# Lookup of gate and up weights: one of the seven comparison masks of a unit moves from VectorE to GpSimd

## What is computed

```python
def _ghost_linear(x, idx, lut):
    w = lut[idx]
    return jnp.einsum('bsh,oh->bso', x, w)
gate = _ghost_linear(x, gate_idx, lut)      # gate_idx, up_idx: (688, 256), values 0 to 15
up = _ghost_linear(x, up_idx, lut)
h = jax.nn.silu(gate) * up
return _ghost_linear(h, down_idx, lut)      # down_idx: (256, 688)
...
x = x + 0.5 * _L0_ffn_ref(_layernorm(x), ...)
x = x + _L0_attn_ref(_layernorm(x), ...)
x = x + 0.5 * _L0_ffn_ref(_layernorm(x), ...)
```

## Time and profile before

| | us |
|---|---|
| median of three runs (533.44 to 533.71) | 533.71 |
| profiled execution, its own time | 530.59 |
| span of the profiled execution | 528.9 |
| DVE busy over the span | 375.0 |
| PE busy over the span | 475.3 |
| POOL busy over the span | 159.0 |
| DVE's first mask starts | 6.80 |
| last matmul of unit 3 ends | 35.98 |

### The profile page before, as it was taken

The page is one execution under the profiler, slowest core; times in us unless marked ns, Lnnn a source line. Parts: engine busy times, 40 slices in busy tenths (PEclk is TensorE's granted clock), DMA queues, the critical chain, the costliest instruction groups (busy, mean ns, idle before and its releaser), DMA issues.

```text
span 528.9 us, 17153 instructions
## 1 busy us (share of the span) xinstructions
PE 475.3 (90%) x7478; PEld 396.0 (75%) x7478; DVE 375.0 (71%) x739; ACT 285.7 (54%) x516; POOL 159.0 (30%) x215
## 2 busy tenths in 40 slices
PE   4999999999989988759889998999978799999996
PEld 3658797988978866647778777877856678898986
DVE  6998836466777998855778887788848856565542
ACT  3658535252447989876556655666545533233241
POOL 1100040204051111116556777656636401000000
PEclk9999999999999999778999999999989999999999
DMA  8950070000000000010000000000340000101011
GB/s 201 235 202 1 1 337 1 1 1 1 0 1 0 2 0 1 20 40 5 4 4 5 4 5 5 5 4 4 147 198 4 2 3 0 41 1 40 1 40 41
DMA packets 7163, 21.31 MB, mean 40 GB/s; under 512 B 688, under 2 KB 5296, under 8 KB 6448
## 3 DMA queue, kind: packets, MB, share of 16 engines
q1 hardware_dynamic: 6688, 18.05, 10.2%
q10 hardware_dynamic: 400, 2.16, 1.8%
HBM read 12.87 MB, written 6.55 MB: 37 GB/s over the span
## 4 chain that ended last, share of the span: by engine, by line
PE 39%; issue 11%; ACT 8%; POOL 7%; DVE 6%; DMA 0%; SPq 0%; POOLq 0%; DVEq 0%; ACTq 0%
POOL w L1229 5%; PE intra L994 4%; DVE cv L640 2%; PE seg L862 2%; ACT cv L678 2%; PE yo L68 2%; PE yo L69 2%; PE yo L70 2%; PE pj L68 1%; PE XB L956 1%; PE pj L70 1%; PE XB L916 1%; PE new L968 1%; PE pj L69 1%; ACT pre L677 1%
## 5 line engine op out<-in xcount | busy, mean ns | idle before, releaser
L1229 POOL TENSOR_TENSOR w<-xdt,ends 32x512 f32<-32x512 f32 (+3 forms) x63 | 66.5, 1074 | 2.8 <-PE prior L963 1.4
L1013 ACT ACTIVATE seg<-seg 128x512 f32<-128x512 f32 x64 | 35.9, 579 | 50.2 <-PE seg L862 50.0
L640 DVE SCALAR_TENSOR_TENSOR cv<-pre,vec,cv 128x512 f32<-128x512 f32 x72 | 52.9, 750 | 2.8 <-ACT cv L678 1.1
L1097 DVE TENSOR_TENSOR mmat<-seg,gs 128x512 f32<-128x512 f32 x64 | 42.5, 684 | 15.8 <-ACT seg L1013 15.8
L514 POOL TENSOR_TENSOR n_rstd<-n_ve,m_half 128x4 f32<-128x4 f32 x12 | 13.0, 1086 | 122.7 <-DVE n_ve L509 122.6
L1033 ACT ACTIVATE xbd<-xdt 32x512 f32<-32x512 f32 x64 | 39.9, 624 | 1.2
L68 PE MATMUL pj<-n_xT,win 128*128 128x512 f32 x88 | 35.6, 404 | 5.0 <-PEq L130 2.3
L994 PE MATMUL intra<-xbd,mmat 128*32 128x32 f32 x2048 | 34.5, 223 | 5.4 <-issue 5.4
L862 PEld LDWEIGHTS seg<-abk,m_seg 96*32 96x32 bf16 x2048 | 21.1, 97 | 23.7 <-DVE mmat L1097 12.8
L994 PEld LDWEIGHTS intra<-xbd,mmat 128*32 128x32 f32 x2048 | 32.2, 152 | 8.2 <-issue 6.2
L1026 ACT ACTIVATE f_hT<-f_h 128x512 fp32r<-128x512 f32 (+1 forms) x24 | 15.2, 632 | 41.0 <-DVE f_h L1108 41.0
(11 more groups left out here) (252 smaller groups left out, 1454.0 us busy)
## 6 DMA issues: line engine op xcount, KB each, us to landing
wgu_dram<-wgu SPq DMA_DIRECT2D x1, 2816.0 KB, 8.2
wgu<-wgu_dram SPq DMA_DIRECT2D x1, 2816.0 KB, 10.5
out<-x_res SPq DMA_DIRECT2D x4, 512.0 KB, 2.9
x_res<-in_x SPq DMA_DIRECT2D x1, 1536.0 KB, 24.0
wd_dram<-wd SPq DMA_DIRECT2D x1, 1536.0 KB, 11.6
wd<-wd_dram SPq DMA_DIRECT2D x1, 1536.0 KB, 13.7
gu_idx<-in_gu ACTq DMA_DIRECT2D x4, 352.0 KB, 8.1
gu_idx<-in_gu SPq DMA_DIRECT2D x4, 352.0 KB, 12.7
```

Source lines behind the costliest of these rows:

```text
L640: dve.scalar_tensor_tensor(dst, pre[:, x, k:k + GN].rearrange("p (t c) -> p t c", c=P), cw[:, x, k:k + 1], dst, ALU.mult, ALU.add).then_in ...
L1013: act.activation(seg[u_ % 2][:, :, :], seg[u_ % 2][:, :, :], ACT.Exp).then_inc(s["exp_ok"], 1)
L1097: dve.tensor_tensor(mmat[a % 2][:, i, :], seg[u_ % 2][:, :, :], gs[a % 2][:, i].unsqueeze(2).broadcast_to([P, IU, HEADS]), ALU.mult).then_ ...
L1229: pool.tensor_tensor(heads(w[r, n, :]), heads(xdt[a % 2][r, :]), ends[a % 2][r, n * HEADS:(n + 1) * HEADS].unsqueeze(2) .broadcast_to([Q * ...
```

## The change

POOL makes the mask of pair 7 in each of the four units, into a buffer of its own, `mask_p`, and DVE makes pairs 1 to 6. DVE's ring shrinks from six buffers to five, so that the memory stays the same. Two semaphores are new: `pmask_ok` (the mask is made) and `pused_ok` (PE is done with it). POOL's first reciprocal root stands behind its mask of unit 1. PE's order of pairs stays 1, ..., 7, 0. The down units are as before.

```diff
-        GU_D, GU_A, DN_D, DN_A = 6, 2, 5, 2
+        GU_D, GU_A, DN_D, DN_A = 5, 2, 5, 2
+        DVE_N = PAIRS - 2
...
+            mask_p = big("mask_p")
...
             pool.wait_ge(half_ok, 1)
-            norm.pool_rstd(pool, 0)
+            for unit in range(QTR):
+                pool.wait_ge(gu_in[unit], 32)
+                if unit:
+                    pool.wait_ge(pused_ok, unit)
+                pool.tensor_scalar(mask_p[:, :], gu_idx[:, unit, :], entry[:, PAIRS - 1:], None, ALU.is_equal
+                                   ).then_inc(pmask_ok, 1)
+                if unit == 1:
+                    norm.pool_rstd(pool, 0)
             pool.wait_ge(aused_ok, QTR)
...
             def masks(unit):
-                for p in range(1, PAIRS):
-                    n = unit * (PAIRS - 1) + p - 1
+                for p in range(1, PAIRS - 1 if unit < QTR else PAIRS):
+                    n = unit * DVE_N + p - 1 if unit < QTR else QTR * DVE_N + (unit - QTR) * (PAIRS - 1) + p - 1
...
                 for p in (*range(1, PAIRS), 0)[first:last]:
-                    if p:
-                        n = unit * (PAIRS - 1) + p - 1
+                    if p == PAIRS - 1 and unit < QTR:
+                        pe.wait_ge(pmask_ok, unit + 1)
+                        mask = mask_p
+                    elif p:
+                        n = unit * DVE_N + p - 1 if unit < QTR else QTR * DVE_N + (unit - QTR) * (PAIRS - 1) + p - 1
                         pe.wait_ge(mask_ok, n + 1)
...
-                    ins.then_inc(used_ok if p else aused_ok, 1)
+                    ins.then_inc(pused_ok if p == PAIRS - 1 and unit < QTR else used_ok if p else aused_ok, 1)
```

More of the change, by code:

```diff
@@ L156, in build_front @@
             "dn_in", "ident_ok", "half_ok", "entry_ok", "zeroed", "hz", "two_ok", "lut_ok", "table_ok"))
-        mask_ok, amask_ok, used_ok, aused_ok, evac_ok, split_hi, wout_s = map(sem, (
-            "mask_ok", "amask_ok", "used_ok", "aused_ok", "evac_ok", "split_hi", "wout_s"))
+        mask_ok, amask_ok, used_ok, aused_ok, evac_ok, split_hi, wout_s, pmask_ok, pused_ok = map(sem, (
+            "mask_ok", "amask_ok", "used_ok", "aused_ok", "evac_ok", "split_hi", "wout_s", "pmask_ok", "pused_ok"))
         gate_ok, up_ok, silu_ok, h_ok, h_hi, h_lo, down_ok, res_ok, stored = map(sem, (
@@ L251, in masks @@
                     else:
-                        m, d = n - QTR * (PAIRS - 1), unit - QTR
-                        dve.wait_ge(used_ok, max(n - DN_D + 1, QTR * (PAIRS - 1)))
+                        m, d = n - QTR * DVE_N, unit - QTR
+                        dve.wait_ge(used_ok, max(n - DN_D + 1, QTR * DVE_N))
                         halves = 2 if d < FCH - 1 else 1
@@ L411, in lookup @@
                 for p in (*range(1, PAIRS), 0)[first:last]:
-                    if p:
-                        n = unit * (PAIRS - 1) + p - 1
+                    if p == PAIRS - 1 and unit < QTR:
[3 more added lines that the diff above has]
+                        n = unit * DVE_N + p - 1 if unit < QTR else QTR * DVE_N + (unit - QTR) * (PAIRS - 1) + p - 1
                         pe.wait_ge(mask_ok, n + 1)
-                        mask = mask_d[n % GU_D] if unit < QTR else low_d[(n - QTR * (PAIRS - 1)) % DN_D]
+                        mask = mask_d[n % GU_D] if unit < QTR else low_d[(n - QTR * DVE_N) % DN_D]
                     else:
```

## The result

| | before | after |
|---|---|---|
| median, us | 533.71 (533.44 to 538.26, 4 runs) | 543.71 (542.56 to 547.05, 4 runs) |
| profiled execution, its own time | 530.59 | 547.05 |
| its span | 528.9 | 545.3 |
| DVE's first mask starts | 6.80 | 6.64 |
| last matmul of unit 3 ends | 35.98 | 48.19 |

The changed kernel is slower, by 1.8%: ratio 1.0177, 95% interval [1.0106, 1.0248]. A second measurement beside the kernel before gave 1.0231 [1.0157, 1.0305]. The median moved by 10.0 us where +4.5 was forecast, and lies 0.4 us above the upper end of the stated range.

The account below looks back on a forecast made before the run. DVE's path from 6.8 to 36 us was taken as the bound. Removing 3.46 us, adding 0.64 on PE and 4 x 1.83 of blocking gave +4.5 us, median 538.2 us; range 534.3 to 543.3.

Parts of the forecast that it names:

- the sum: Whole kernel: four blocked masks at 1.83 us each, less 2.8 us saved, give +4.5 us.
- X: Length of one POOL mask, 128x1408 from integers to fp32r: 2.1 us, between 1.43 and 3.38.
- The bound: Front from 6.8 to 36 us: DVE's path sets the pace; four masks removed save 3.46 us.
- the tail: End of unit 3: PE multiplies three masks instead of two after DVE's last, 0.64 us more.
- Blocking: DVE's masks beside POOL: DVE stands still until POOL's instruction is over; price 1.83 us a mask, between 1.16 and 3.11.
- Rival A: POOL and DVE masks run without blocking: unit 3 ends near 33.2, -2.8 us, 530.9; chance 11%.
- Rival B: Three of four POOL masks block, or X at its short end: +2.7, +0.7 or +1.8 us; chance about 22% together.
- The price B = X - 0.27: DVE's loss per POOL mask: X less 0.15 start-up, plus 0.75, less 0.865; 1.83 us.
- All four meet: Units 0 to 3: each POOL mask falls among DVE's masks; the shorter ring of five hides.
- POOL's turn: POOL among DVE's masks waits only until the running mask ends; read from a root taking 1.62 us, usually 1.02.
- Rival D: POOL gets no turn until DVE stops at the ring's end; PE waits for pair 7: about +6 us; chance 2%.
- Rival C: PE falls to its slow pace in units 2 and 3: about +3 us on top, 541; 7%, with long X 15%.

Follow-up runs that it names:

- the kernel with one ACT mask: Kernel before, with pair 0 moved earlier in unit 3 and ACT making pair 7's mask in unit 2 by two activations: ratio 0.9974.
- the second profile: The changed kernel measured again without any edit, beside the kernel before: 544.36 us against 533.48, ratio 1.0231.
- the kernel with the busy PE: Changed kernel, plus 15 matmuls of 512 columns on PE ahead of its wait for pair 5 of unit 2: 545.88 us, ratio 1.0284.
- extra masks: Kernel before with a ring of five; DVE keeps seven masks, POOL also makes pair 7's into an unread buffer: 543.78 us against 533.48, ratio 1.0209.
- clears: As the kernel with extra masks, but POOL clears 128x1408 instead of comparing: 534.06 us against 533.48, ratio 1.0021.
- 640 columns: Kernel before with a ring of five; POOL compares 640 columns of unit 1 into an unread buffer beside the statistics: ratio 1.0030.
- all columns: As the kernel with 640 columns, but POOL compares all 1408 columns: 534.82 us in one run, against 533.84 for the kernel before.
- order: Kernel before, with PE taking pair 0 first in unit 3 and pairs 1 to 7 behind it: ratio 0.9986.
- two: As the kernel with one ACT mask, but ACT makes pair 7's mask of unit 1 too: ratio 0.9934 against the kernel before.

## Why the prediction was right and where it was wrong

The direction and the mechanism were right, the size was not: +10.0 us where the sum gave +4.5. The median came out near the upper end of the range, but that end was built from X = 3.38 with a blocking price of 3.11 us, and X proved longer still; that the total lies only 0.4 us beyond it is partly luck, since the sum with the measured price is larger than the move of the median.

**The bound.** Right. DVE's path set the front, a mask taken off it was worth 0.865 us (0.86 in the kernel with one ACT mask), and the tail was 0.64 us longer (2.24 against 1.60 us in the second profile).

**Blocking.** Right, and the main thing. The stretched down mask found in the trace of before was the same mechanism. The runs show it four ways: with nothing saved (+14.1 us for four meetings), with a clear in place of the comparison (about 1.1 us for 1.27), with none beside the statistics, and with none when ACT makes the mask. They agree with the rule of the Trainium skill named in the prediction (SBUF — State Buffer, "Who interferes with whom"): DVE's masks, whose pace is that of the faster form, stop, and the statistics over one tensor don't. The prediction counts the 1.216 us of `u` as agreeing with that rule too; but `u` reads two tensors, a form that a POOL clear left alone (0.69 us beside it) while a POOL multiplication, which reads, stretched it. So the two forms of DVE's instructions aren't stopped by the same things; for `u` the cause is argued from one row. Rival A, no blocking, is out.

**The length X: this is the term that was mis-sized.** I took 2.1 us, with 3.38 as the most; it is 3.92. Two inferences failed. I took a clear's pace for the elements of a `tensor_scalar`, and the only row of one has 32 elements, which holds nothing of the slope. And I took the pace of two-tensor operations for the upper end, on the ground that this one reads only one tensor: 2.31 ns an element there, 2.66 here. The surcharge for fp32r output that I read from two groups (0.46 ns an element) isn't there for this operation: 0.08 us over 1408 elements are 0.06 ns. Rival B's short end, X = 1.43, falls with the same run. So does the estimate of 1.4 us that the prediction worked out from the Trainium skill (GPSIMD Engine Reference, "Performance versus the Vector engine" and its selection table): there one-input operations are roughly at line rate, here the comparison takes 3.92 us and 2.66 ns an element, and the measurement decides.

**The price B = X - 0.27.** Nearly right: 1.00 forecast for the clear of 1.27 us, 1.02 to 1.13 measured; 3.65 for 3.92 us, 3.5 measured. The term of 0.15 us in it, POOL's start-up that is over by its turn, was an estimate that no row showed by itself. With the measured B the sum is 4 x 3.5 - 2.8 = +11.2 us. The second profile has 47.47 - 35.98 = +11.5 at unit 3, the first +12.2 with the clock's share.

**All four meet.** Right in the changed kernel. The ring of five cost nothing in units 0 to 2; in unit 3, with PE at the lower clock, DVE waited 0.25 us (0.36 in the second profile) for a buffer that PE hadn't freed.

**POOL's turn.** Wrong. I read from one row of 1.62 us that POOL waits only until the running mask ends. The clear waited 4.0 us, the mask in the kernel with the busy PE 8.39 - 3.92 = 4.5 us. In unit 3 of the changed kernel POOL got its turn where DVE paused for the buffer: its own 3.92 us reach back from 44.23 to 40.31, DVE's fifth mask ends at 40.53 and the sixth starts at 40.77. With PE kept busy that pause is gone, and so is POOL's turn. Rival D had the mechanism, though its price was taken for a full stop in each unit. It changes who waits more than how much is lost.

**PE's pace.** Rival C, given 15% together with a long X, came true in part: X lay beyond its long end, and the clock fell in both profiles. I had held against it that the clock stayed up after a pause of 1.27 us; with one of 3.46 us it didn't. The first drop is all but hidden behind DVE, the second costs 0.97 + 0.38 = 1.35 us where it happens; the +3 us that the rival put on it is more than was seen.

**What the total adds.** From the first L68 matmul to the end the profiles take 488.7 us (before), 492.6 and 493.1 (changed, twice), 489.5 (extra masks), 490.8 (clears), 490.2 (640 columns), 491.0 (all columns), 492.4 (busy PE), 488.7 (order), 491.6 (one ACT mask) and 491.1 us (two). This part is the same work in all. What makes the 4 us stays open. The spans of one kernel vary as much, the shorter ones mostly at a higher mean granted clock: those of the kernel before, measured beside the second run of the change, reach from 526.1 us at 0.983 to 533.9 us at 0.974. Of the 16.4 us between the profiled pair 12.6 lie ahead of that matmul and 3.8 behind it; the medians are 10 us apart, so the totals don't confirm the sum of the front more closely than by a few us.

## What to carry over

An elementwise operation moved from VectorE to GpSimd didn't run beside VectorE's masks, which go in its faster form (one tensor read, 1.6 elements a ns): each GpSimd instruction stopped them for about its own length (3.5 us for 3.92, 1.1 us for 1.27). So compare GpSimd's length with VectorE's for the same operation (3.92 against 0.865 us here), not GpSimd's idle time with the need. Look in the trace of before for VectorE instructions far over their group's median with a GpSimd instruction beside them; they show the stop and its price. If work must leave VectorE, give it to an engine that doesn't stop it: ScalarE needed two instructions for the mask, and the first such mask still saved 0.86 us. GpSimd's comparison cost nothing only beside the statistics.

Take the per-element pace of an operation from two rows of that operation with different sizes, never from another operation's slope and this one's intercept.

## What was unexpected of the hardware

- `tensor_scalar` on GpSimd took 2.66 ns an element (int32 to fp32r), more than the 2.31 of an operation on two tensors with fp32r output; with other types, a multiplication or a constant it was within 0.16 us of the same 3.92.
- A `tensor_scalar` of four elements on VectorE took 2.22 us in place of 0.17 beside GpSimd's mask, while aggregates as small kept their length.
- A GpSimd clear stopped VectorE's masks (1.1 us for 1.27), and left an operation of VectorE on two tensors at its 0.69 us.
- A GpSimd comparison issued among VectorE's masks waited between 0.6 and 4.9 us for its turn; the clears waited once 4.0 us and otherwise not at all. Which mask is stopped wasn't predictable from the order.
- TensorE's granted clock fell from the 2.4 to the 1.2 GHz level in part of 28 to 44 us (mean 0.77 and 0.80) during a pause of 3.46 us, in both profiles of the changed kernel, and stayed up when TensorE was kept at work there.
